# A fused state-space and expert kernel: the first block's taps move to the row queue, GpSimd takes part of the first statistics, and the first centring moves ahead of the reciprocal

## The chip, the cores and the metric

The kernel runs on one core of one Trainium2 chip. The metric is the time of one execution on the device in microseconds, as the median of several runs. The core has five instruction streams that matter here: TensorE (PE, with its weight loads as PEld), VectorE (DVE), ScalarE (ACT), GpSimd (POOL) and SyncE (SP). They wait for each other through semaphores only. DMA transfers are issued by SP, ACT and POOL, each into a queue of its own, and are carried out by 16 DMA engines.

## The reference

The input x has 8 sequences of 4096 positions with 512 channels, in float32. Two residual layers follow each other:

```
x = x + attn(layernorm(x))      # a causal convolution along the sequence, per channel, plus x * omega
x = x + ffn(layernorm(x))       # eight low-rank experts with an exact gelu, two picked for each token
```

The convolution's taps are worked out from five small parameter arrays (delta, alpha, beta, gamma, omega). A layer norm subtracts the row's mean and divides by the square root of its variance plus 1e-5. The kernel needs the first layer norm's mean and variance of all 32768 rows, while it then works through the channels 16 at a time. The stretch before that work can begin is what this document is about.

## The kernel before

The rows stand in SBUF as 128 positions within a chunk (partitions) by 256 (sequence, chunk) pairs by channels. The kernel goes through them in two halves g = 0 and 1 of 128 pairs each. A half has 32 blocks i of 16 channels, a block two units k of 8 channels; eight blocks make a tile of 128 channels. Between the halves lies the expert stage.

**The front part** ends when PE starts the first unit of g = 0. Four things happen in it side by side.

- SP loads the first 128 pairs with all 512 channels as 64 row loads of 512 KB (two pairs each, line 717, the first eight at line 700) into a ring of eight buffers. Row load n is issued once both readers have freed buffer n - 8: DVE's `bn_stats` (line 1103, two for each load, semaphore `s_free`) and POOL's copy of the first 128 channels, `keep(n)` (line 458, `s_keep`).
- ACT and PE work out 32 tables of taps and decays, which ACT stores to `taps_d` and `decay_d` in DRAM (lines 913 and 915). When the last has landed, ACT itself issues two loads for block 0: the taps (line 936, 256 KB, into `wide`) and the decays (line 937, 128 KB, into `dk`). For the later blocks `load_weights` does this on SP (lines 735 and 737).
- POOL works out the rest of the routing (`routing_rest`, three small instructions after each `keep` from n = 16 on) and issues eight of 64 tiny scatters (`send`, line 466) after the odd n from 49 to 63.
- DVE turns the 128 columns of `bn_stats` results into mean and variance: `statistics`, eight dependent instructions (lines 1144 to 1151, semaphore `s_dv`).

**What follows in order on each engine.** On ACT: `reverse(0, 0, 0)` and `reverse(0, 1, 0)`, two copies each (lines 975 and 976), which wait for block 0's taps; `lower(0, 0, 0)` (line 982); a dummy square root that loads the table (line 998); `deviations(0)`, the square root over the variances (line 941, after `s_dv` has reached 8); a dummy that loads the exponential's table (line 1000); then the first `carry` (line 952) and, once PE's first product is there, `shift_s` (line 956). ACT takes them strictly in that order:

```
            act.wait_ge(s_late, NLATE)
            for k in range(2):
                reverse(0, k, 0)
            lower(0, 0, 0)
            act.activation(spare[:, 1:2], eps[:], ACT.Sqrt)
            deviations(0)
```

On DVE: the reciprocal of the deviations (line 1226), `centre(0, 0, 0)` (line 1235, DVE's half of subtracting the mean; POOL does the other half at line 582), `stage(0, 0, 0)` (line 1246, times the reciprocal), then `centre(0, 0, 1)`, `stage(0, 0, 1)`, `centre(0, 1, 0)` and the first scan (line 1273). On PE: `chunk` (line 1458), `local` (line 1471), and from the second unit on `between` (line 1483). `stage` of unit u waits until `local` of unit u - 2 has finished with the buffer. On POOL: the first `centre`, `place_decays(0)` (line 535, waits for block 0's decays), a `send`, the second `centre`, the clearing of a buffer and another `send`, then the third `centre`, which also waits for the first scan. On SP: once the last `keep` is done, taps and decays of blocks 1 to 4, the decays of block 4 after `place_decays(0)`, and behind them the loads of the next tile (line 680).

Of the kernel before, what the change touches and what calls it, by code (L numbers as in the profile page):

```python
# [16 lines left out]
ALU = mybir.AluOpType  # L17
# [3 lines left out]
P = 128  # L21
# [27 lines left out]
def build(nc, x, delta, alpha, beta, gamma, omega, ew, ei, w1a, w1b, w2a, w2b, out, ei_experts=8):  # L49
    B, L, D = x.shape  # L50
# [10 lines left out]
    NK = D // KD  # L61
    SB = KD // 2
# [5 lines left out]
    LR = 2  # L68
    LBUF = 8
    TB = 4  # L70
    WB = 4
    NL = P // LR
# [38 lines left out]
    with ctx:  # L111
# [3 lines left out]
        def sem(name):  # L115
            return ctx.enter_context(nc.semaphore(name))
# [74 lines left out]
        w1bs = wb_row[:, KC * ER:].rearrange("p (k f) -> p k f", k=2)  # L191
        act_h = cen_row.rearrange("p (k f t) -> p k f t", k=2, t=QT)
# [72 lines left out]
        s_dv = sem("s_dv")  # L265
        s_std = sem("s_std")
# [63 lines left out]
        DV_STATS = 9  # L330
        SENT = 8
# [64 lines left out]
        def _(pool):  # L396
# [118 lines left out]

            rest = routing_rest()
            for n in range(NL):
                keep(n)
                if n == LBUF - 1:
                    pool.memset(wb[:, 0, :, :, 0:2 * ZR], 0.0).then_inc(s_late, 1)  # L520
                    pool.memset(near[:], 0.0).then_inc(s_late, 1)
                    pool.memset(shift_s[:], 0.0).then_inc(s_late, 1)
                if n >= 2 * LBUF:
                    for _ in range(3):
                        next(rest, None)
                if n >= NL - 2 * SENT and n % 2 == 1:
                    send((n - (NL - 2 * SENT)) // 2)

# [139 lines left out]
        def _(sp):  # L668
# [50 lines left out]
            sp.wait_ge(s_keep, NL)  # L719
# [80 lines left out]
            def tiles(g):  # L800
                t0 = g * DG
                if g == 0:
                    for k in range(1, WB):
                        load_weights(k, k)
                tile(g, t0, True, False)
                for t in range(t0 + 1, t0 + DG - 1):
                    tile(g, t, False, False)
                tile(g, t0 + DG - 1, False, True)
# [70 lines left out]
        def _(act):  # L879
# [49 lines left out]
            act.wait_ge(s_tab, 16)  # L929
            for k in range(TB):  # L930
                act.wait_ge(s_tapd[k], 16 * (NK // TB))
            act.wait_ge(s_dec, 16 * NK)
            for k in range(1):
                row = taps_d[k:k + 1].rearrange("k s i d -> k (s i d)")
                src = bass.AP(row.tensor, row.offset, [[2, ZR], [2 * (P + ZR), SB], [1, 2 * P]])
                act.dma_start(taps_in[k * ZR:(k + 1) * ZR], src).then_inc(s_w[k], 16)
                act.dma_start(dk[:, k, :], decay_d[k:k + 1].rearrange("k s n d -> (k s) (n d)")).then_inc(s_dk[k], 16)

            def deviations(g):
                act.wait_ge(s_dv, (g + 1) * DV_STATS - 1)  # L940
                act.activation(rstd[:, g * P:(g + 1) * P], var[:, g * P:(g + 1) * P], ACT.Sqrt,
                               bias=eps[:, 0:1]).then_inc(s_std, 1)
# [149 lines left out]
        def _(dve):  # L1092

            stats1 = wb_row[:, KC * ER:KC * ER + 6 * P].rearrange("p (r f) -> p r f", f=6)

# [36 lines left out]
            def statistics(g, st_of):  # L1132
# [9 lines left out]
                st = st_of.rearrange("p r f -> p f r")  # L1142
                m, v, r = (a[:, g * P:(g + 1) * P] for a in (mean, var, rstd))
# [79 lines left out]
            for _ in statistics(0, stats1):  # L1223
                pass
            dve.wait_ge(s_std, 1)
            dve.reciprocal(rstd[:, 0:P], rstd[:, 0:P]).then_inc(s_dv, 1)
            dve.wait_ge(s_dv, DV_STATS)

# [58 lines left out]
            dve.wait_ge(s_late, NLATE)  # L1287
            centre(0, 0, 0)
            stage(0, 0, 0)
# [354 lines left out]
```

## Time and profile before

| | us |
|---|---|
| median of 3 runs | 1125.89 |
| lowest and highest | 1124.06, 1131.58 |
| the profiled execution's own time | 1135.82 |
| its span | 1134.0 |
| first `local` product of PE begins at | 116.18 |

A time in a row is counted from the span's start. In the timeline a row gives start, duration, engine, line, operation, what is written from what, and in brackets how long the engine sat idle before and what ended that. A `q` behind an engine's name marks its sequencer, which issues DMA transfers.

### The profile page before, as it was taken

What the parts mean: (1) busy time and instruction counts of PE and PEld (TensorE: products, weight loads), DVE (VectorE), ACT (ScalarE), POOL (GpSimd) and SP (SyncE); (2) the same over time, 40 slices, a digit from 0 to 9 for tenths busy, and PEclk for the clock granted to TensorE, in tenths of its full rate; (3) what the DMA queues carried; (4) which work ended last, traced back from release to release, by engine and by line L of the source; (5) the groups of instructions that cost most, each with busy time, mean ns of one, the idle gap of its engine ahead of it and who ended that gap; (6) DMA issues with size and microseconds to landing.
All of it is one profiled execution on the core that took longest, in us unless ns stands there. A gap on an engine that the chain in (4) does not pass through costs nothing. (4 is left out here: it accounts for less than half of the span.)

```text
span 1134.0 us, 32989 instructions
## 1 busy us (share of the span) xinstructions
PE 930.9 (82%) x11452; PEld 750.8 (66%) x11452; DVE 817.4 (72%) x1360; ACT 783.8 (69%) x1151; POOL 605.4 (53%) x706
## 2 busy tenths in 40 slices
PE   3760888888688689999999999999988888886882
PEld 2540776767577567777777777777767777775771
DVE  7978998979689324576766666766757989896891
ACT  3872898979689544656565656565667989897890
POOL 5625986858483225566566656665655323332330
PEclk9995999989989898999999999999998999899896
DMA  9998999999999794999998879898839999999976
GB/s 319 394 401 298 260 248 241 274 233 295 289 295 317 217 277 110 278 258 293 264 271 221 236 207 234 228 232 218 207 80 267 231 220 273 244 308 291 307 173 150
DMA packets 392137, 288.01 MB, mean 254 GB/s; under 512 B 125928, under 2 KB 339592, under 8 KB 391554
## 3 DMA queue, kind: packets, MB, share of 16 engines
q1 hardware_dynamic: 348098, 212.21, 69.8%
q0 software_dynamic: 19520, 36.26, 14.6%
q10 hardware_dynamic: 24448, 38.61, 10.1%
q8 instruction: 43, 0.70, 0.3%
q14 instruction: 28, 0.23, 0.1%
HBM read 197.41 MB, written 100.61 MB: 263 GB/s over the span
## 5 line engine op out<-in xcount | busy, mean ns | idle before, releaser
L1471 PE MATMUL ps<-xn,wb 128*128 128x128 f32 x2048 | 275.7, 290 | 0.0
L1071 ACT ACTIVATE cen<-ps 128x1024 f32<-128x1024 f32 x156 | 155.9, 1023 | 168.8 <-PE ps L1566 161.6
L1471 PEld LDWEIGHTS ps<-xn,wb 128*128 128x128 f32 x2048 | 250.7, 200 | 17.4 <-issue 3.1
L582 POOL TENSOR_TENSOR cen<-xb,mean 128x512 f32<-128x512 f32 x128 | 142.9, 1117 | 219.4 <-DVE state L1273 166.7
L1246 DVE TENSOR_TENSOR xn<-cen,rstd 128x1024 f32<-128x1024 f32 x128 | 174.5, 1363 | 49.1 <-POOL cen L582 37.9
L1566 PE MATMUL ps<-carry,wb 64*128 64x256 f32 x1248 | 172.6, 402 | 16.0 <-DVE carry L1319 8.5
L1458 PE MATMUL ps<-xn,near 128*32 128x128 f32 x2048 | 87.9, 292 | 117.7 <-DVE xn L1246 71.9
L1581 PE MATMUL ps<-cen,xn 128*64 128x128 f32 x2496 | 160.9, 276 | 1.9 <-ACT cen L1071 1.8
L1581 PEld LDWEIGHTS ps<-cen,xn 128*64 128x64 f32 x2496 | 136.2, 137 | 39.3 <-ACT cen L1071 28.0
L1257 DVE TENSOR_TENSOR xb<-xb,ps 128x1024 f32 (+1 forms) x128 | 152.9, 1195 | 8.3 <-PE ps L1483 8.3
L975 ACT ACTIVATE wb<-wide 32x1024 f32<-32x1024 f32 x126 | 144.4, 1146 | 15.5 <-DMA wide<-taps_d 12.9
L1566 PEld LDWEIGHTS ps<-carry,wb 64*128 64x128 f32 x1248 | 116.3, 190 | 46.5 <-issue 36.0
L1458 PEld LDWEIGHTS ps<-xn,near 128*32 128x32 f32 x2048 | 52.8, 114 | 140.9 <-issue 66.7
L976 ACT ACTIVATE wb<-wide 32x768 f32<-32x768 f32 x126 | 114.8, 911 | 1.5
L614 POOL DMA_INDIRECT wide<-y_d,pick_g x78 | 86.9, 1114 | 46.6 <-POOL pick_g L611 34.6
L466 POOL DMA_INDIRECT slot_d<-rowf,posi x64 | 104.7, 1636 | 11.9 <-issue 11.9
L1303 DVE BATCH_NORM_STATS2 tstat<-wide 128x6 f32<-128x512 f32 x78 | 53.1, 690 | 76.0 <-DMA wide<-y_d,pick_g 75.4
L1235 DVE TENSOR_TENSOR cen<-xb,mean 128x512 f32<-128x512 f32 x128 | 90.2, 704 | 12.4 <-DMA xb<-L_attn_x 12.3
L1483 PE MATMUL ps<-state,carry 32*128 32x128 f32 x2048 | 94.2, 298 | 0.0
L1103 DVE BATCH_NORM_STATS2 wb<-xb 128x512 f32 (+1 forms) x128 | 80.0, 682 | 17.9 <-DMA xb<-L_attn_x 17.2
L1483 PEld LDWEIGHTS ps<-state,carry 32*128 32x128 f32 x2048 | 69.7, 188 | 25.7 <-issue 24.7
L956 ACT ACTIVATE shift_s<-ps,coef 128x124 f32<-128x124 f32 x128 | 45.4, 355 | 57.8 <-PE ps L1458 56.8
(173 smaller groups left out, 1272.6 us busy)
## 6 DMA issues: line engine op xcount, KB each, us to landing
xb<-L_attn_x SPq DMA_DIRECT2D x160, 512.0 KB, 10.1
out<-xb SPq DMA_DIRECT2D x72, 512.0 KB, 6.3
xb<-L_attn_x ACTq DMA_DIRECT2D x128, 256.0 KB
out<-xb SPq DMA_DIRECT2D x88, 256.0 KB, 4.6
wb<-L_ffn_w_B SPq DMA_DIRECT2D x78, 256.0 KB
wide<-taps_d SPq DMA_DIRECT2D x63, 256.0 KB
dk<-decay_d SPq DMA_DIRECT2D x63, 128.0 KB
out<-y_d SPq DMA_DIRECT2D x4, 1536.0 KB, 12.8
```

The lines of the kernel that those rows point to most:

```text
L466: pool.indirect_dma_start(out=slot_d, out_offset=bass.IndirectOffsetOnAxis(ap=pos_col[:, c:c + 1], axis=0), in_=row_col[:, 2 * c:2 * c + 2 ...
L582: pool.tensor_tensor(cen[:, k, 0:QB // 2].rearrange("p b r d -> p r b d"), unit_view(pool, g, i, k)[:, :, 0:UC // 2] .rearrange("p r (b d) ...
L975: act.activation(dst[0:ZR], src, ACT.Copy)
L976: act.activation(dst[ZR:2 * ZR, :, :, ZR:P], src[:, :, :, 0:P - ZR], ACT.Copy).then_inc(s_rev, 1)
L1071: act.activation(act_h[:, b % 2].rearrange("p f t -> p (f t)"), ps[:, 2 * (b % 2):2 * (b % 2) + 2, :].rearrange("p a t -> p (a t)"), ACT.G ...
L1246: dve.tensor_tensor(xn[:, k].rearrange("p (b d) r -> p b d r", d=2), cen[:, k].rearrange("p b r d -> p b d r"), rstd[:, g * P:(g + 1) * P] ...
L1257: dve.tensor_tensor(view, view, ps[:, QB * k:QB * k + QB, 0:2 * P] .rearrange("p b (d r) -> p r b d", d=2), ALU.add).then_inc(s_ev, 1)
L1458: ins = pe.matmul(ps[b * 2 * N:(b + 1) * 2 * N, QB * k, 2 * P:3 * P], near[:, h, k * QB + b, d:d + 2, :].rearrange("p z n -> p (z n)"), xn ...
L1471: ins = pe.matmul(ps[:, QB * k + b, d * P:(d + 1) * P], wb[:, h, k * QB + b, d, :], xn[:, k, 2 * b + d, :], start=(b > 0 and d == 0), stop ...
L1483: ins = pe.matmul(ps[:, QB * k + b, d * P:(d + 1) * P], carry[rows, k, d * P:(d + 1) * P], state[rows, k, :], start=False, stop=True, skip ...
L1566: ins = pe.matmul(ps[:, 2 * (b % 2) + h, f * QT:(f + 1) * QT].rearrange("p (a t) -> p a t", a=2), w1bs[half_rows, k, c * P:(c + 1) * P], r ...
L1581: ins = pe.matmul(ps[h * RANK:(h + 1) * RANK, 4, 0:P], w2as[:, (f // 2) * (FC // 2) + 2 * b + f % 2, :], act_h[:, b % 2, f, side * P:(side ...
```

## The change

It does four things. ACT no longer issues block 0's two loads; SP's `load_weights` takes block 0 too, and SP no longer waits for the last `keep` before the four pairs of loads but behind them, in front of the next tile's loads. POOL does the eight instructions of the statistics for the first 112 pairs (`first_rows`, after `keep(58)`), and DVE's `statistics(0)` covers the last 16. The eight scatters move from after the odd n of 49 to 63 to after the odd n of 41 to 55. On DVE `centre(0, 0, 0)` stands in front of the wait for the square root and the reciprocal. ACT's square root waits for `first_rows` too.

```diff
+        NHALF = 8
+        SPL = 7 * P // 8
+        SEND0 = 5 * NL // 8
...
+            def first_rows():
...
+                st = stats1[:, 0:SPL, :].rearrange("p r f -> p f r")
+                m, v, r = (a[:, 0:SPL] for a in (mean, var, rstd))
+                pool.wait_ge(s_free, SPL // LR)
+                chain(pool.tensor_tensor(m, st[:, 1, :], st[:, 4, :], ALU.add))
+                chain(pool.tensor_scalar(m, m, 0.5, None, ALU.mult))
+                chain(pool.tensor_tensor(r, st[:, 1, :], st[:, 4, :], ALU.subtract))
+                chain(pool.tensor_tensor(r, r, r, ALU.mult))
+                chain(pool.tensor_scalar(r, r, D / 4.0, None, ALU.mult))
+                chain(pool.tensor_tensor(r, r, st[:, 2, :], ALU.add))
+                chain(pool.tensor_tensor(r, r, st[:, 5, :], ALU.add))
+                chain(pool.tensor_scalar(v, r, 1.0 / D, None, ALU.mult))
...
             for n in range(NL):
                 keep(n)
+                if n == SPL // LR + 2:
+                    first_rows()
...
-                if n >= NL - 2 * SENT and n % 2 == 1:
-                    send((n - (NL - 2 * SENT)) // 2)
+                if SEND0 <= n < SEND0 + 2 * SENT and n % 2 == 1:
+                    send((n - SEND0) // 2)
...
-            sp.wait_ge(s_keep, NL)
             for k in range(TB):
                 sp.wait_ge(s_tapd[k], 16 * (NK // TB))
...
                 if g == 0:
-                    for k in range(1, WB):
+                    for k in range(WB):
                         load_weights(k, k)
+                    sp.wait_ge(s_keep, NL)
...
-            act.wait_ge(s_tab, 16)
-            for k in range(TB):
-                act.wait_ge(s_tapd[k], 16 * (NK // TB))
-            act.wait_ge(s_dec, 16 * NK)
-            for k in range(1):
-                row = taps_d[k:k + 1].rearrange("k s i d -> k (s i d)")
-                src = bass.AP(row.tensor, row.offset, [[2, ZR], [2 * (P + ZR), SB], [1, 2 * P]])
-                act.dma_start(taps_in[k * ZR:(k + 1) * ZR], src).then_inc(s_w[k], 16)
-                act.dma_start(dk[:, k, :], decay_d[k:k + 1].rearrange("k s n d -> (k s) (n d)")).then_inc(s_dk[k], 16)
...
             def deviations(g):
                 act.wait_ge(s_dv, (g + 1) * DV_STATS - 1)
+                if g == 0:
+                    act.wait_ge(s_half, NHALF)
...
-            for _ in statistics(0, stats1):
+            for _ in statistics(0, stats1, SPL):
                 pass
-            dve.wait_ge(s_std, 1)
-            dve.reciprocal(rstd[:, 0:P], rstd[:, 0:P]).then_inc(s_dv, 1)
-            dve.wait_ge(s_dv, DV_STATS)
...
+            dve.wait_ge(s_half, NHALF)
             centre(0, 0, 0)
+            dve.wait_ge(s_std, 1)
+            dve.reciprocal(rstd[:, 0:P], rstd[:, 0:P]).then_inc(s_dv, 1)
+            dve.wait_ge(s_dv, DV_STATS)
             stage(0, 0, 0)
```

## Rows read from the trace of the kernel before

**Rows 1.** The page, part 1: busy time, share of the span and instructions.

```profile
PE 930.9 (82%) x11452; PEld 750.8 (66%) x11452; DVE 817.4 (72%) x1360; ACT 783.8 (69%) x1151; POOL 605.4 (53%) x706
```

**Rows 2.** Busy time by windows, 100 to 110 us; last three columns: PEclk, DMA share, GB/s.

```profile
100.00:110.00 10.00, 0.00 (x0) 0.00 (x0) 9.50 (x19) 2.90 (x4) 6.25 (x10) 0.50 0.58 197
```

**Rows 3.** Waits: ACT from 80 to 125 us, DVE from 110 to 360 us.

```profile
ACT wb L975 <- DMA wide<-taps_d: 12.9, 1, 12.9
ACT rstd L941 <- DVE var L1151: 8.4, 1, 8.4
...
DVE cen L1235 <- DMA xb<-L_attn_x: 6.7, 1, 6.7
```

**Rows 4.** Timeline of ACT at the end of the front part.

```profile
89.73 0.33 ACTq L936 DMA_DIRECT2D wide<-taps_d  x1
...
96.69 1.13 ACT L975 ACTIVATE wb<-wide 32x1024 f32<-32x1024 f32 x1 [12.93 <-DMA wide<-taps_d]
...
102.75 0.20 ACT L998 ACTIVATE spare<-eps 128x1 f32<-128x1 f32 x1
...
111.32 0.40 ACT L941 ACTIVATE rstd<-var,eps 128x128 f32<-128x128 f32 x1 [8.37 <-DVE var L1151]
```

**Rows 5.** Timeline of DVE in the same stretch.

```profile
102.19 6.31 DVE L1103 BATCH_NORM_STATS2 wb<-xb 128x512 f32 x10 [0.25 <-DMA xb<-L_attn_x]
...
108.54 0.38 DVE L1144 TENSOR_TENSOR mean<-wb 128x128 f32<-128x128 f32 x1
...
111.06 0.23 DVE L1151 TENSOR_SCALAR var<-rstd 128x128 f32<-128x128 f32 x1
...
111.82 0.95 DVE L1226 RECIPROCAL rstd<-rstd 128x128 f32<-128x128 f32 x1 [0.54 <-ACT rstd L941]
...
113.69 1.22 DVE L1246 TENSOR_TENSOR xn<-cen,rstd 128x1024 f32<-128x1024 f32 x1
...
114.83 1.58 DVE L1235 TENSOR_TENSOR cen<-xb,mean 128x512 f32<-128x512 f32 x1
...
118.20 0.42 DVE L1273 TENSOR_TENSOR_SCAN state<-carry,shift_s 128x128 f32<-128x128 f32 x1
...
120.00 1.51 DVE L1246 TENSOR_TENSOR xn<-cen,rstd 128x1024 f32<-128x1024 f32 x1 [1.38 <-POOL cen L582]
```

**Rows 6.** Timeline of PE in its first and second unit.

```profile
115.17 1.08 PE L1458 MATMUL ps<-xn,near 128*32 128x128 f32 x16 [33.82 <-DVE xn L1246]
...
116.18 3.25 PE L1471 MATMUL ps<-xn,wb 128*128 128x128 f32 x16
...
120.59 2.05 PE L1471 MATMUL ps<-xn,wb 128*128 128x128 f32 x16
```

**Rows 7.** Timeline of POOL: a routing sum, a scatter, the last keep, two centrings.

```profile
35.53 0.46 POOL L486 TENSOR_TENSOR carry<-carry 128x128 f32<-128x128 f32 x1 [4.40 <-DVE xn L1212]
...
105.25 0.97 POOL L466 DMA_INDIRECT slot_d<-rowf,posi  x1 [0.32 <-issue]
...
107.12 0.40 POOL L458 COPY xb<-xb 128x256 f32<-128x256 f32 x1 [0.48 <-DMA xb<-L_attn_x]
...
111.46 1.10 POOL L582 TENSOR_TENSOR cen<-xb,mean 128x512 f32<-128x512 f32 x1 [2.65 <-DVE var L1151]
...
118.77 1.09 POOL L582 TENSOR_TENSOR cen<-xb,mean 128x512 f32<-128x512 f32 x1 [0.23 <-DVE state L1273]
```

**Rows 8.** DMA, 88 to 98 us: ACT's queue (packets, MB, share of 16 engines); row loads.

```profile
q10 hardware_dynamic: 508, 0.47, 15.7%
...
xb<-L_attn_x SPq DMA_DIRECT2D x6, 512.0 KB, 10.0
```

**Rows 9.** DMA, 107.5 to 113.5 us: packets, MB and rate.

```profile
DMA packets 1277, 1.19 MB, mean 198 GB/s; under 512 B 120, under 2 KB 1277, under 8 KB 1277
```

**Rows 10.** Timeline of SP: the last row loads, and the next tile's first loads.

```profile
80.94 17.09 SPq L717 DMA_DIRECT2D xb<-L_attn_x  x11
...
113.49 4.39 SPq L680 DMA_DIRECT2D xb<-L_attn_x  x4
```

More of the change, by code:

```diff
@@ L191, in build @@
         w1bs = wb_row[:, KC * ER:].rearrange("p (k f) -> p k f", k=2)
+        stats1 = wb_row[:, KC * ER:KC * ER + 6 * P].rearrange("p (r f) -> p r f", f=6)
         act_h = cen_row.rearrange("p (k f t) -> p k f t", k=2, t=QT)
@@ L265, in build @@
         s_dv = sem("s_dv")
+        s_half = sem("s_half")
         s_std = sem("s_std")
@@ L514, in routing_rest, with chain @@
                 assert n == NROUTE, n
+            def first_rows():
+                n = 0
+                def chain(ins):
+                    nonlocal n
+                    n += 1
+                    ins.then_inc(s_half, 1)
+                    pool.wait_ge(s_half, n)
+                st = stats1[:, 0:SPL, :].rearrange("p r f -> p f r")
[9 more added lines that the diff above has]
+                chain(pool.tensor_scalar(v, r, 1.0 / D, None, ALU.mult))
+                assert n == NHALF, n
             rest = routing_rest()
@@ L1092, in _ @@
         def _(dve):
-            stats1 = wb_row[:, KC * ER:KC * ER + 6 * P].rearrange("p (r f) -> p r f", f=6)
             def row_stats(q, bufs=range(LBUF)):
@@ L1130, in keep2, with statistics @@
                                 ring2[:, i:i + 2, 0:P]).then_inc(s_free2, 1)
-            def statistics(g, st_of):
+            def statistics(g, st_of, r0=0):
                 n = g * DV_STATS
@@ L1140, in chain @@
                     dve.wait_ge(s_dv, n)
-                st = st_of.rearrange("p r f -> p f r")
-                m, v, r = (a[:, g * P:(g + 1) * P] for a in (mean, var, rstd))
+                st = st_of[:, r0:, :].rearrange("p r f -> p f r")
+                m, v, r = (a[:, g * P + r0:(g + 1) * P] for a in (mean, var, rstd))
                 yield chain(dve.tensor_tensor(m, st[:, 1, :], st[:, 4, :], ALU.add))
```

## The prediction

> **What bounds the kernel now.** I began with the page. PE is busy for 82% of the span and no engine is above that [rows 1], so the long stages are loops in which engines take turns, and the change doesn't touch them. It touches the stretch before PE's first product, in which PE waits: what counts is how early that product and the loop behind it begin.
>
> The windows come next. From 100 to 110 us DVE is busy for 9.5 of 10 us, PE for none, and the DMA share has dropped to 0.58 [rows 2]: the row loads run out in this window. The waits then say who holds whom. ACT waited 12.9 us for block 0's taps and later 8.4 us for the variances [rows 3]. Both are idle time of an engine that wasn't the bound: ACT had slack of 8.4 us. The timelines give the chain that set the end. The last row load landed at 107.12, when POOL's last keep could start [rows 7]. DVE's last five loads took it from 102.19 to 108.50 without a pause, the eight statistics instructions to 111.29, ACT's square root came at 111.32, the reciprocal ended at 112.77, the first `stage` began at 113.69 [rows 4, 5], PE's `chunk` at 115.17 and its `local` at 116.18 [rows 6]. The rule of the old chain is rows, statistics, root, reciprocal, centring, stage. What the taps do is not on it: ACT got them at 96.69 and had finished everything in front of the square root at 102.95 [rows 4].
>
> **The change part by part.**
>
> *Block 0's taps behind the rows.* This is the part that decides. The last row load is issued at about 98.0 (80.94 plus 17.09) [rows 10], and in SP's queue the taps come next. Row loads land 10.0 us after their issue (median), with eight in the queue [rows 8], so what is put behind them waits for them. Two numbers are needed, when the rows end and how long the taps take after that. Taking the 384 KB of taps and decays out from between the rows gives the rows time back: ACT's queue held 15.7% of the 16 engines over 10 us, that is 1.57 us, for 0.47 MB of which this pair is 0.39 [rows 8], so 1.3 us, 1.6 at most. I take 1.4: the rows end at 105.7. The taps are two thirds of the pair, 0.9 us by the same row and 1.3 us at the 198 GB/s of the stretch that held mostly such transfers (256 KB by 198; its first microsecond was nearly empty, so this is a bound from above) [rows 9]. I take 1.0. The taps land at 106.7, with 105.9 and 107.6 as the nearer bounds.
>
> From there ACT's order counts. From the first `reverse` to the end of the dummy square root it took 102.95 minus 96.69, 6.26 us [rows 4], and the diff leaves that order alone. So the square root can't start before 106.7 + 6.3 = 113.0, against 111.32 before: 1.7 us later. ACT's 8.4 us of slack are used up and the taps are now on the chain.
>
> *Statistics.* On DVE eight instructions over 128 columns took 2.75 us (108.54 to 111.29) [rows 5]; over 16 columns they take between nothing and that. DVE's last `bn_stats` ends 1.4 us after the last row, at 107.1, so the variances stand between 107.1 and 109.9. Either is more than 3 us before 113.0: whatever is saved here, up to 2.75 us, is worth nothing, since ACT isn't there yet. If the taps were early it would be worth all of it.
>
> *POOL's eight instructions.* The trace shows none of this form. The nearest is a two-input sum of 128 elements at 0.46 us [rows 7]; with an estimated 0.08 us between dependent ones I take 0.54 each and 4.3 us in all. From above, the centring of 512 elements takes 1.10 us [rows 7], so 8.8 us. From below, 0: the work is wholly added on POOL, so a gain is excluded. `first_rows` starts after `keep(58)`, five loads before the last, at about 99.5, and ends at 103.8; queued behind it are five keeps of 0.4 us, done at 106.2 after the last row. Nobody waits for these five but the first centrings and SP's next tile. At 8.8 us the keeps end at 110.4, and POOL's centring (1.1 us) at 111.5, still ahead of the first `stage` at 114.5. The cover is ACT's chain; POOL's addition costs something from about 11 us on. The Trainium skill, GPSIMD Engine Reference, section Engine selection, puts two-input elementwise work on GpSimd at about twice VectorE's time. By that the five two-input instructions would take 0.76 us each from DVE's 0.38 [rows 5] and the eight together some 6 us, which the same cover hides. The trace has 0.46 against 0.38 for as many elements [rows 5, 7], nearer to equal, so I stay with 4.3; no sum here depends on it.
>
> *The new waits.* ACT waits for POOL's part, ready at 103.8 to 108.3; behind it stand the square root and the first `carry`, which ACT reaches at 113.0. DVE waits for it before the first centring. Neither costs anything.
>
> *The eight scatters* take 0.97 us each on POOL [rows 7]. Moved earlier by eight loads, they each delay one keep by about a microsecond; a buffer comes free only with DVE's two `bn_stats` as well, which end some 1.3 us after the landing (6.31 us for five loads [rows 5]). So the row loads are not held up. Gone from POOL's tail, they make room for `first_rows`. The last scatter also stood between the last keep and the centring, a place that waited for the variances anyway. Nothing.
>
> *First centring ahead of the reciprocal.* Before, root to stage was 111.32 to 113.69, 2.37 us. Now only the root with its hand-over (0.50), the reciprocal (0.95) and a gap of 0.04 are left, 1.49 us [rows 4, 5]: the centring, which filled nearly all of the 0.92 us between the reciprocal's end and the `stage`, is done while DVE waits for ACT. A gain of 0.9 us.
>
> *SP.* It issues its eight transfers from 96.6 on, not behind the last keep, and none of them stands in front of a row. The wait for the last keep now stands before the next tile's loads, which began at 113.49 [rows 10] behind `place_decays(0)`; that comes about 1.5 us earlier. The only long wait of DVE for such loads up to 360 us is one of 6.7 us [rows 3], two tiles later and behind a release that moves with the loop, so this is worth nothing.
>
> **The sum.** First `stage` at 113.0 + 1.5 = 114.5, that is +0.8 us. PE's first `chunk` and `local` follow by as much: `local` runs 3.25 us (this is at a granted clock of 0.50, the 1.2 GHz level, after 33.8 us of idleness; the same 16 products later take 2.05) [rows 2, 6] and ends at 120.2. But the loop didn't hang on PE there. DVE's second centring took 1.58 us beside POOL's [rows 5], where the changed POOL is done before, so it should fit into the 0.9 us that the first one had. DVE then reaches the first scan at about 118.3, near the old 118.20. POOL's third centring follows it at 118.8 and ends at 119.9, as before [rows 7]. The third `stage` stood at 120.00 [rows 5], held by that centring; it must also wait for `local`, now 120.2. So of +0.8 us at the first product +0.2 us is left in the loop, and nothing later takes or gives more. The profiled execution (1135.82, span 1134.0) would become 1136.0. It is 9.9 us above the median; nothing in the front part depends on that, so I put the same +0.2 on the median: 1126.1 us.
>
> **Rivals.**
> - *The taps come early.* If they don't wait for the rows, they land as ACT's did, 7.0 us after their issue [rows 4], at about 103.6. The root starts at 109.9, the variances' upper bound, and the third `stage` about 2.4 us earlier: 1123.5. For it speaks that a transfer of ACT's overtook row loads queued before it; against it, that this was another queue. The Trainium skill, DMA: Bandwidth & Descriptors, section Queues, rings and completion order, has each engine switch between queues, but take one queue's descriptors in ring order. That speaks for the forecast; this trace shows the overtaking between queues only.
> - *The rows gain nothing, the slower side.* If rows end at 107.1 as before, because the last engines to finish had other small work, the taps land at 108.1, the root starts at 114.4, PE's first `local` ends at 121.6 and the third `stage` slips by 1.6 us: 1127.5. It decides from a landing past 106.7 on, each microsecond costing one. For it speaks that the DMA share is only 0.58 in the last window [rows 2], so some engines lag, whatever lies between.
> - *The loop settles otherwise.* A shifted start meets the tile loads at another phase; the one 6.7 us wait [rows 3] could grow or shrink by some 4 us: 1122 or 1130.
> - *Over 1%.* None of the mechanisms reaches 11 us. All of the front part's waits at stake add up to less than 9.
>
> **How the numbers follow.** Forecast (landing 105.9 to 107.6, from -0.6 to +1.1 us) 55%, taps early 14%, rows gain nothing 17%, loop otherwise 11% (half each way), over 1% 3%. About 1% is what a measurement of this kernel can tell from no change. The range takes in the first three cases with the spread of the runs shown (1.8 below the median and 5.7 above) and part of the fourth: 1122.5 to 1130.0. Faster by over 1%: 0.01; within 1%: 0.97; slower: 0.02.
>
> **What would show it.** In the profile after: ACT's first line 975 waits for the taps until 106 to 107.6 and the square root starts 6.3 us behind; DVE's last statistics end before 110 and DVE then sits idle for 3 us or more until the reciprocal; POOL's eight instructions take 4 to 9 us and nobody waits; root to `stage` 1.5 us; PE's first `chunk` between 115.2 and 117. I am wrong if line 975 starts before 105, if POOL's centring is what the first `stage` waits for, or if the loop's start and the total move by different amounts.

## The result

The changed kernel is slower by half a per cent: 1131.91 us against 1126.95 us (medians of 20 runs each), ratio 1.0051 with a 95% interval from 1.0037 to 1.0064. In microseconds the ratio is +5.7, from 4.2 to 7.2; the two medians are 5.0 apart. I had forecast +0.2 us and a range whose upper end, 1130.0, the median has left.

The profiled execution of the changed kernel has a span of 1129.4 us, less than the 1134.0 of before. Single executions differ by more than the effect: the stretch of the experts between the halves alone is some 12 us shorter in this execution than in that of before (432 against 444 us, by the first and last of their products). So the two spans can't be compared, but the front parts can, step by step. The timeline of ACT in the changed kernel, in the form of [rows 4]:

```profile
110.73 1.13 ACT L997 ACTIVATE wb<-wide 32x1024 f32<-32x1024 f32 x1 [28.24 <-DMA wide<-taps_d]
...
116.80 0.20 ACT L1020 ACTIVATE spare<-eps 128x1 f32<-128x1 f32 x1
116.91 0.39 ACT L963 ACTIVATE rstd<-var,eps 128x128 f32<-128x128 f32 x1
```

Block 0's taps let ACT begin at 110.73, where I had 106.7 and where 96.69 stood before [rows 4]. From there to the end of the dummy square root it is 6.27 us, as forecast, and the root starts at 116.91, 5.6 us later than before. DVE in the same stretch, in the form of [rows 5]:

```profile
110.10 1.29 DVE L1123 BATCH_NORM_STATS2 wb<-xb 128x512 f32 x2 [0.89 <-DMA xb<-L_attn_x]
...
112.93 0.17 DVE L1171 TENSOR_SCALAR var<-rstd 128x16 f32<-128x16 f32 x1
113.14 0.69 DVE L1252 TENSOR_TENSOR cen<-xb,mean 128x512 f32<-128x512 f32 x1
...
117.33 0.95 DVE L1308 RECIPROCAL rstd<-rstd 128x128 f32<-128x128 f32 x1 [3.50 <-ACT rstd L963]
...
118.32 1.22 DVE L1263 TENSOR_TENSOR xn<-cen,rstd 128x1024 f32<-128x1024 f32 x1
...
124.52 1.23 DVE L1263 TENSOR_TENSOR xn<-cen,rstd 128x1024 f32<-128x1024 f32 x1 [2.18 <-PE ps L1492]
```

The statistics are done at 113.10 and DVE then waits 3.5 us for ACT's root. The first `stage` is 4.63 us late and the third, from which the loop runs, 4.52 us. But the last `bn_stats` pair also starts only at 110.10: the rows themselves are late. POOL shows that best, since its keep of a row load starts as the load lands:

```profile
85.39 0.40 POOL L463 COPY xb<-xb 128x256 f32<-128x256 f32 x1
...
105.58 0.40 POOL L463 COPY xb<-xb 128x256 f32<-128x256 f32 x1 [0.38 <-DMA xb<-L_attn_x]
...
107.83 0.40 POOL L463 COPY xb<-xb 128x256 f32<-128x256 f32 x1 [1.85 <-DMA xb<-L_attn_x]
...
110.00 0.40 POOL L463 COPY xb<-xb 128x256 f32<-128x256 f32 x1 [1.77 <-DMA xb<-L_attn_x]
```

The first of these is keep 48, the last keep 63. Before, the last one started at 107.12 [rows 7]; I had put it at 105.7. The last three are 2.2 us apart, where DVE's five loads of [rows 5] had come every 1.26 us. So two things went wrong at once: the rows end 4.3 us later than forecast, and the taps behind them with them.

### The profile page after: what moved, and what is told of

Read it like the earlier page. It is cut to its first block and busy times, and to the rows that moved or that the text cites. A ratio compares the mean times of both kernels' runs of the same rounds, so it can differ in the third digit from the quotient of the medians.

```text
span 1129.4 us, 32996 instructions
## 1 busy us (share of the span) xinstructions
PE 925.3 (82%) x11452; PEld 748.0 (66%) x11452; DVE 814.9 (72%) x1360; ACT 786.2 (70%) x1151; POOL 605.5 (54%) x714
## 5 line engine op out<-in xcount | busy, mean ns | idle before, releaser
L1587 PE MATMUL ps<-carry,wb 64*128 64x256 f32 x1248 | 170.0, 402 | 12.8 <-DVE carry L1340 12.2
L1587 PEld LDWEIGHTS ps<-carry,wb 64*128 64x128 f32 x1248 | 113.3, 190 | 42.7 <-issue 23.6
L471 POOL DMA_INDIRECT slot_d<-rowf,posi x64 | 96.9, 1514 | 11.9 <-issue 11.9
```

What stands on the lines that cost most here:

```text
L471: pool.indirect_dma_start(out=slot_d, out_offset=bass.IndirectOffsetOnAxis(ap=pos_col[:, c:c + 1], axis=0), in_=row_col[:, 2 * c:2 * c + 2 ...
L1587: ins = pe.matmul(ps[:, 2 * (b % 2) + h, f * QT:(f + 1) * QT].rearrange("p (a t) -> p a t", a=2), w1bs[half_rows, k, c * P:(c + 1) * P], r ...
```

## The experiments

Theory 1, crowding: not all DMA engines finish the rows at the same time. Those that are done go on to the four pairs of taps and decays in the same queue, and in doing so slow down the row packets of those that lag. Theory 2: the rows are late because of another part of the change, the earlier scatters or POOL's eight instructions. Behind both stands what I had forecast, the place of the taps in the queue and ACT's order.

What makes theory 1 possible is seen in the kernel before. Its DMA from 102 to 109 us, in 40 slices of 0.175 us (busy tenths, then rate):

```profile
DMA  9999997644433343222222112101000000000663
GB/s 410 410 374 352 375 340 293 247 165 176 164 141 118 120 142 129 94 94 94 105 82 82 70 70 82 59 0 5 2 0 0 0 0 0 0 0 0 105 47 111
DMA packets 583, 0.89 MB, mean 126 GB/s; under 512 B 130, under 2 KB 175, under 8 KB 583
## 3 DMA queue, kind: packets, MB, share of 16 engines
q1 hardware_dynamic: 487, 0.88, 35.9%
q0 software_dynamic: 96, 0.00, 1.1%
```

From 103.2 on, the share falls step by step. It is down to 0.4 at 103.4, while the last packet of a row starts at 106.5 and the last row load lands just before 107.12. So most engines are done some three microseconds before the last one. In the changed kernel the same stretch reads:

```profile
DMA  9999998999999999999999999999999999999986
GB/s 187 164 164 164 123 158 146 222 310 269 193 158 181 158 158 135 181 199 205 193 240 275 240 240 205 217 199 240 222 263 252 217 228 228 211 211 211 170 164 146
DMA packets 1302, 1.41 MB, mean 201 GB/s; under 512 B 101, under 2 KB 1128, under 8 KB 1302
## 3 DMA queue, kind: packets, MB, share of 16 engines
q1 hardware_dynamic: 1302, 1.41, 109.0%
```

All engines are busy, at half the rate that they had a moment before (381 GB/s from 98 to 100 us). A packet took 1.09 x 16 x 7.0 us / 1302 = 94 ns in the mean for 1.08 KB; before, the same sum (with both queues' 37.0%) gives 71 ns for 1.53 KB. Packets that carry less take longer: the engines are held up within them. The trace also keeps each packet with its size: a row goes in packets of 2 KB, taps and decays in packets of 1 KB. In the changed kernel the first packet of 1 KB behind the rows starts at 100.9 us and the last one of a row at 108.8, so the two do run side by side. And a row packet between 102 and 109 us took 162 ns in the mean, against 86 ns before.

**The front part's own spread.** Single profiles are compared below, so the kernel before was profiled once more.

> The kernel before, profiled once more, to learn how far the front part itself differs between two executions. If the rows' supply is steady, keep 48 starts at 84.4 and the last keep at 107.1 as in the first profile, within 0.3 us; if it is not, every comparison of single front parts carries that spread (the four kernels above had keep 48 at 84.8 to 85.5), and the distance from keep 48 to the last keep, 22.8 us before, is the better measure of crowding.

Its keep 48 started at 85.54 and its last keep at 108.16, both one microsecond later than in the first profile, and its third `stage` at 121.04. The distance between the two keeps was 22.62 us against 22.76. So times of single front parts carry about 1 us, and the distance from keep 48 to the last keep is what crowding is read from.

**Block 0 back on ACT.** The changed kernel with:

```diff
+            sp.wait_ge(s_keep, NL)               # ahead of SP's pairs, as before
...
-                    for k in range(WB):
+                    for k in range(1, WB):
                         load_weights(k, k)
-                    sp.wait_ge(s_keep, NL)
...
+                act.dma_start(taps_in[k * ZR:(k + 1) * ZR], src).then_inc(s_w[k], 16)
+                act.dma_start(dk[:, k, :], ...).then_inc(s_dk[k], 16)
```

> The changed kernel with one part undone: ACT issues block 0's taps and decays again as soon as the tables have landed, and SP waits for the last keep before the pairs of blocks 1 to 3. POOL's 112 columns, the earlier scatters and the first centring ahead of the reciprocal stay. Theory 1 (crowding: the four pairs queued behind the rows run on the DMA engines that have finished their rows and slow down the engines that lag): the last keep starts at 106.5 to 107.3 as before, ACT's first line 975 at 96 to 98, the variances stand at 110.3, the square root follows at once, the first stage at 111.8 (1.9 us earlier than before), and the total is 1.5 to 2.5 us below before (ratio 0.998). Theory 2 (the rows end late because of the earlier scatters or POOL's statistics): the last keep stays at 109 to 110, the first stage comes at 114 or later, total 0 to 1 us above before.

The distance was 22.48 us, so theory 2 falls: the earlier scatters and POOL's instructions are all in this kernel and the rows come as before. The variances decided again and the root followed them at once:

```profile
111.15 0.40 ACT L973 ACTIVATE rstd<-var,eps 128x128 f32<-128x128 f32 x1 [8.75 <-DVE var L1181]
```

The first `stage` was 0.76 us earlier than before in a front part whose rows came 1.2 us later. Against keep 48 that is a gain of 1.9 us, but at the third `stage` only 1.0 us of it is left, because the second `stage` had to wait for POOL's second centring. In the total nothing shows: ratio 1.0011, from 0.9988 to 1.0034. I had expected 1.5 to 2.5 us below before, and the interval holds 1.4 us at most: that forecast failed.

**One pair behind the rows.** The changed kernel with:

```diff
-                    for k in range(WB):
+                    load_weights(0, 0)
+                    sp.wait_ge(s_keep, NL)
+                    for k in range(1, WB):
                         load_weights(k, k)
-                    sp.wait_ge(s_keep, NL)
```

> The changed kernel with only block 0's pair queued directly behind the rows; SP waits for the last keep before the pairs of blocks 1 to 3. Theory 1, with the crowding done by the three pairs that nobody needs yet: the last keep at 106 to 107, the taps at 107 to 108, the square root 6.3 us later at 113.3 to 114.3, the third stage 0 to 1 us later than before, total 0 to 1.5 us above before. If block 0's pair alone does the crowding, or theory 2 holds: the last keep at 109 or later, taps at 110 or later, the third stage 3 us or more later, total 3 to 5 us above before.

The last keep came at 107.36, the distance was 22.52 us, ACT began at 108.25 and the root at 114.42. The third `stage` was 1.4 us later than in the first profile of before and 0.4 us later than in the second; the ratio was 1.0027, from 1.0002 to 1.0052. I had expected the last keep by 107, the third `stage` at most 1 us later and the total at most 1.5 above before (measured +3.0, from 0.2 to 5.9), so all came out on the far side. The three pairs that nobody needs yet account for 2.1 us of the changed kernel's distance. But block 0's pair alone already used up what taking it from between the rows gives back: the distance is that of before, not 1.4 us less. This is, nearly to the number, the rival that the rows gain nothing.

**This part alone.** The kernel before with ACT's two loads removed, all four pairs on SP and the wait for the last keep behind them:

```diff
-            sp.wait_ge(s_keep, NL)
...
-                    for k in range(1, WB):
+                    for k in range(WB):
                         load_weights(k, k)
+                    sp.wait_ge(s_keep, NL)
```

> The kernel before with only this part of the change: all four pairs on SP directly behind the rows, the wait for the last keep behind them. DVE does all 128 columns, the scatters stay at n = 49 to 63, the centring stays behind the reciprocal. Theory 1: the last keep at 109.5 to 110.5, taps at 110.5 to 111.5, the square root at 117 to 118, the first stage at 119.3 to 120.3 (0.9 later than in the changed kernel), the total 5 to 7 us above before (ratio 1.005 to 1.006). Theory 2: the last keep at about 105.7, the taps at 107, the total 1 to 2 us above before.

Last keep 110.42, distance 24.99 us, ACT from 111.66, root at 117.84, first `stage` at 120.04, ratio 1.0060 (1.0037 to 1.0083). That is within or next to every bound that I had set. The taps' place by itself gives the whole loss. At the third `stage`, 126.36 against 124.52 in the changed kernel, the other parts of the change give 1.8 us back by single profiles; in the total the two intervals overlap, and no gain of theirs is shown.

**Three pairs behind the rows, block 0 on ACT.** This has the crowding without the late taps:

```diff
+                act.dma_start(...)               # block 0's two loads, on ACT as before
...
-                    for k in range(WB):
+                    for k in range(1, WB):
                         load_weights(k, k)
                     sp.wait_ge(s_keep, NL)
```

> The changed kernel with block 0's pair on ACT again, but the pairs of blocks 1 to 3 still queued directly behind the rows. It separates crowding from the lateness of the taps. Theory 1: the last keep at 108.5 to 110 although the taps come at 97; ACT is ready at 103, so the variances decide: the square root at 111.7 to 113, the first stage at 113.2 to 114.5, total -0.5 to +1 us against before. Without crowding it is the same as the kernel with all of SP's pairs behind the keep: last keep at 107, first stage at 111.8, 2 us below before.

```profile
96.04 1.13 ACT L1007 ACTIVATE wb<-wide 32x1024 f32<-32x1024 f32 x1 [13.01 <-DMA wide<-taps_d]
...
114.13 0.40 ACT L973 ACTIVATE rstd<-var,eps 128x128 f32<-128x128 f32 x1 [11.82 <-DVE var L1181]
```

ACT had its taps at 96.04 and waited 11.8 us for the variances: the last keep started at 110.98, 25.68 us after keep 48. Both were later than my bounds. The distance is 3.2 us more than in the first experiment, from which this kernel differs only in SP's wait. The ratio was 1.0041, from 1.0021 to 1.0061. I had expected the total between 0.5 below and 1 us above before; it was +4.6, from 2.4 to 6.9. Crowding alone, without late taps, costs nearly as much as the whole change.

**What crowds.** The taps differ from the rows in three ways: all engines read the same 10 KB of DRAM over and over, a piece is 1 KB, and a transfer is written into 32 partitions only. Four kernels take these apart. The first reads other data:

```diff
-                    for k in range(WB):
-                        load_weights(k, k)
+                    for k in range(WB):          # 256 KB each out of x, every KB once
+                        far_src = bass.AP(x.tensor, 7 * L * D + k * ZR * SB * 2 * P, ...)
+                        sp.dma_start(taps_in[k * ZR:(k + 1) * ZR], far_src).then_inc(s_w[k], 16)
+                        sp.dma_start(dk[:, k, :], dec).then_inc(s_dk[k], 16)
```

> The changed kernel, but the four taps transfers behind the rows read 256 KB each from a far part of x, every KB once, instead of the overlapping windows over 10 KB that make up a block's taps. Sizes, destinations and order stay. Block 0 to 3 of the first half then get wrong taps: that part of the computation is left out. Theory 1a (what crowds the lagging rows is that all engines read the same few KB of DRAM at once): from keep 48 to the last keep 20.5 to 22.5 us (after: 24.6), the stretch from 101 to 109 moves 300 GB/s or more at a DMA share of 1.0 until the fast engines are done, the taps land at 107 to 108 and the square root comes 2 to 3 us earlier than in the changed kernel. Theory 1b (it is the size of 1 KB or the 32 partitions written): nothing changes, 24 to 25 us and about 220 GB/s.

It got worse, not better: distance 25.59 us, last keep 111.71, ACT from 112.40. It also changed more than I had meant. The windows lie side by side in x and went as packets of 8 KB, as this line from 102 to 109 us shows (663 packets, 578 of them under 8 KB):

```profile
DMA packets 663, 1.41 MB, mean 201 GB/s; under 512 B 91, under 2 KB 368, under 8 KB 578
```

So neither the shared source nor the small piece is needed for crowding. The second loads the decays behind the rows and the taps after the last keep:

```diff
                     for k in range(WB):
-                        load_weights(k, k)
+                        sp.dma_start(dk[:, k, :], dec).then_inc(s_dk[k], 16)
                     sp.wait_ge(s_keep, NL)
+                    for k in range(WB):
+                        sp.dma_start(taps_in[k * ZR:(k + 1) * ZR], src).then_inc(s_w[k], 16)
```

> The changed kernel with only the four decay transfers (128 KB each, every KB read once, all 128 partitions written, also in pieces of 1 KB) directly behind the rows, and the four taps transfers after the last keep. Theory 1a: decays don't crowd; from keep 48 to the last keep 20.5 to 22 us, the last keep at 105.5 to 106.5; the taps of block 0 are issued after it and land some 2.7 us later at 108.5 to 109.5, the square root 6.3 us behind, the third stage 1.5 to 2.5 us later than before. If the piece size of 1 KB does the crowding, the distance is 23 us or more.

The distance was 20.80 us, 1.9 us less than before: with no taps anywhere near the rows, they end that much sooner. The last keep itself started at 107.30 and not at 105.5 to 106.5, as keep 48 was late too (86.50). The taps, now issued after it, let ACT start 3.8 us behind it and not 2.7, so the third `stage` came 4.3 us later than in the first profile of before, where I had 1.5 to 2.5. The mean packet from 102 to 109 us, from these two lines, took 0.483 x 16 x 7.0 / 915 = 59 ns for 1.26 KB:

```profile
DMA packets 915, 1.15 MB, mean 164 GB/s; under 512 B 93, under 2 KB 617, under 8 KB 915
## 3 DMA queue, kind: packets, MB, share of 16 engines
q1 hardware_dynamic: 913, 1.15, 48.3%
```

A row packet took 86 ns in the mean, as in the kernel before. So pieces of 1 KB don't crowd either. The third is this kernel with the decays' transfers reading the taps' overlapping windows:

```diff
-                sp.dma_start(dk[:, k, :], dec).then_inc(s_dk[k], 16)
+                hot_src = bass.AP(row.tensor, row.offset, [[2, P], [1, 2 * P]])
+                sp.dma_start(dk[:, k, :], hot_src).then_inc(s_dk[k], 16)
```

> The kernel of the decays-early experiment with one thing changed: the four transfers behind the rows (128 KB each, 128 partitions written) now read overlapping windows of 1 KB out of a block's 10 KB of taps, as the taps transfers do. The decays of blocks 0 to 3 of the first half are wrong with it: that part is left out. Reading the same few KB against reading apart, with the partitions written held at 128. If only the 32 partitions of the destination crowd (theory 1c): as with the decays, 20.8 us from keep 48 to the last keep and row packets as before. If the shared source has a part of its own: 22 us or more.

20.93 us: reading the same few KB costs the rows nothing. (These 128 windows, 8 bytes apart, lie within 2 KB of a block's taps, closer together than those of the taps transfers, which cover 10 KB.) The fourth is the kernel with another source, its megabyte sent as one transfer over 128 partitions instead of four over 32:

```diff
-                        sp.dma_start(taps_in[k * ZR:(k + 1) * ZR], far_src).then_inc(s_w[k], 16)
+                    sp.dma_start(taps_in, all_src).then_inc(s_w[0], 16)
```

Three transfers of 0.2 KB after the last keep take over the semaphores of blocks 1 to 3.

> The experiment with another source (four transfers of 256 KB out of x into 32 partitions each) with one thing changed: the same megabyte into the same places as one transfer over all 128 partitions, ahead of the decays. The taps of blocks 0 to 3 of the first half stay wrong: that part is left out. Theory 1c (a transfer into 32 partitions can only use part of the way into SBUF, all engines press on it, and the lagging row packets that need the same part wait): from keep 48 to the last keep 20.5 to 22 us instead of 25.6, and the window 102 to 109 moves 260 GB/s or more instead of 201. If the amount of data behind the rows does the crowding, whatever its shape: 25 us again.

The distance fell from 25.59 to 21.05 us. From 102 to 109 us, the windows of the two (last three columns: clock, DMA share, GB/s), four transfers first:

```profile
102.00:109.00 7.00, 0.00 (x0) 0.00 (x0) 3.70 (x6) 0.00 (x0) 3.98 (x9) 0.50 1.06 201
```

```profile
102.00:109.00 7.00, 0.00 (x0) 0.00 (x0) 6.51 (x16) 0.34 (x1) 3.76 (x9) 0.50 0.70 267
```

Its packets in the same window, 119 of them of 8 KB:

```profile
DMA packets 894, 1.87 MB, mean 267 GB/s; under 512 B 92, under 2 KB 588, under 8 KB 775
```

The same bytes from the same place to the same place: with one transfer the DMA engines moved a third more in two thirds of the busy time, and DVE was busy for 6.51 of 7 us instead of 3.70. The packets themselves say it most directly. In this window a row packet took 175 ns in the mean beside the four transfers and 88 ns beside the one, which is what it takes undisturbed; a packet of 8 KB took 643 ns and 316 ns. Besides the width, two things differ: the four transfers became one, and it stands ahead of all decays. The decays of the second kernel are four transfers in a row over 128 partitions and slowed no row packet, so their number isn't it. What crowds is that a transfer writes into 32 partitions. The Trainium skill, SBUF — State Buffer, section Door 1: the DMA port swizzle, states that partitions 0 to 31, and 0 to 63 as well, are reached through 8 of 16 ports only, about 218 GB/s at best. The 201 GB/s here agree with it. Its rule is what I had not weighed: blocks 0 and 1 lie in partitions 0 to 63, and by it the lagging rows' packets into those have to pass the same ports. That this is what slows the rows is not shown. A packet's record doesn't name its partitions, and in the kernel with one pair all 78 row packets that start between 102.0 and 103.5 us took 122 ns or more, though only block 0's 32 partitions were being written narrowly there.

**A version that keeps what is good.** In the first experiment POOL's second centring held the second `stage`. Two more scatters ahead should clear it:

```diff
-        SENT = 8
-        SEND0 = 5 * NL // 8
+        SENT = 10
+        SEND0 = 9 * NL // 16
```

> The changed kernel with block 0's taps on ACT and SP's wait as before (as the first experiment here), and two more scatters moved ahead: ten after the odd n of 37 to 55, so that POOL has none between its first two centrings. In the first experiment POOL's second centring was what the second stage waited for (1.6 us) and it gave back the 0.8 us won at the first stage. Expected: POOL's second centring ends 1.2 us or more before the second stage needs it, the third stage 0.8 to 1.5 us earlier than in the first experiment, total 0.5 to 1.5 us below it and 0 to 1.5 us below before (ratio 0.999 to 1.000). If the third stage hangs on local's end (PE at half clock), the gain is 0.5 us at most.

```profile
113.33 1.85 POOL L471 DMA_INDIRECT slot_d<-rowf,posi  x1 [0.16 <-issue]
...
115.21 1.11 POOL L612 TENSOR_TENSOR cen<-xb,mean 128x512 f32<-128x512 f32 x1
...
116.42 1.23 DVE L1273 TENSOR_TENSOR xn<-cen,rstd 128x1024 f32<-128x1024 f32 x1 [1.57 <-POOL cen L612]
```

It didn't: the loop of POOL's first centrings issues a scatter of its own between them, whichever number it bears, and the second `stage` waited 1.57 us for POOL as in the first experiment. Moving the start of the list only changes which scatter that is. I had read the code wrongly. The third `stage`, at 119.97, came 0.2 us earlier than in the first experiment and not 0.8 to 1.5. Ratio 1.0001, from 0.9981 to 1.0021.

The last version adds what the decays showed, all four decay transfers behind the rows:

```diff
-            sp.wait_ge(s_keep, NL)
...
-                act.dma_start(dk[:, k, :], ...)      # block 0's decays leave ACT
...
-                    for k in range(1, WB):
-                        load_weights(k, k)
+                    for k in range(WB):
+                        sp.dma_start(dk[:, k, :], dec).then_inc(s_dk[k], 16)
+                    sp.wait_ge(s_keep, NL)
+                    for k in range(1, WB):
+                        sp.dma_start(taps_in[k * ZR:(k + 1) * ZR], src).then_inc(s_w[k], 16)
```

> A version that keeps what the runs speak for: block 0's taps on ACT between the rows, all four decay transfers on SP directly behind the rows (they did not crowd), the taps of blocks 1 to 3 after the last keep, ten scatters ahead, POOL's 112 columns and the first centring ahead of the reciprocal. Expected: from keep 48 to the last keep 22.0 us instead of 22.4 (128 KB less between the rows), everything up to the third stage 0.3 to 0.6 us earlier than with ten scatters alone, the total 0 to 1.5 us below before (ratio 0.9985 to 1.000). If the decays of block 0 land too late for POOL's second centring, the third stage comes no earlier and the ratio is 1.000.

The distance was 22.28 us (22.40 with ten scatters alone), the root started at 110.62 and the third `stage` at 119.60, 0.4 us earlier than in the first profile of before. The ratio was 1.0001, from 0.9967 to 1.0035. Its interval ends just below the one of the changed kernel, which begins at 1.0037. So it is better than the changed kernel and not told apart from the kernel before; nothing tried here is shown to beat that one.

All front parts together (us from the span's start; "ACT's first 975" is the first `reverse`, line 975 of the kernel before; the distance is from keep 48 to the last keep; ratios where several rounds were run):

| kernel | keep 48 | last keep | distance | ACT's first 975 | root | third stage | ratio |
|---|---|---|---|---|---|---|---|
| before | 84.36 | 107.12 | 22.76 | 96.69 | 111.32 | 120.00 | |
| before, again | 85.54 | 108.16 | 22.62 | 96.29 | 112.36 | 121.04 | |
| changed | 85.39 | 110.00 | 24.61 | 110.73 | 116.91 | 124.52 | 1.0051 |
| block 0 on ACT | 85.53 | 108.01 | 22.48 | 96.14 | 111.15 | 120.14 | 1.0011 |
| one pair behind | 84.84 | 107.36 | 22.52 | 108.25 | 114.42 | 121.43 | 1.0027 |
| this part alone | 85.43 | 110.42 | 24.99 | 111.66 | 117.84 | 126.36 | 1.0060 |
| three pairs behind | 85.30 | 110.98 | 25.68 | 96.04 | 114.13 | 123.12 | 1.0041 |
| other source | 86.12 | 111.71 | 25.59 | 112.40 | 118.58 | 125.64 | |
| decays behind | 86.50 | 107.30 | 20.80 | 111.11 | 117.28 | 124.28 | |
| shared source, 128 partitions | 85.26 | 106.19 | 20.93 | 109.84 | 116.02 | 122.98 | |
| one transfer, 128 partitions | 85.11 | 106.16 | 21.05 | 108.66 | 114.83 | 122.54 | |
| ten scatters | 85.44 | 107.84 | 22.40 | 95.93 | 110.98 | 119.97 | 1.0001 |
| decays behind, ten scatters | 85.19 | 107.47 | 22.28 | 94.82 | 110.62 | 119.60 | 1.0001 |

## Why the prediction was wrong

**The step that failed** is the one on SP: that its eight transfers begin early and "none of them stands in front of a row". In the order of the queue that is so. But a queue is served by 16 engines that aren't at the same place in it, and a transfer behind the rows runs beside the lagging rows as soon as the first engine is through. I had the sign of this in hand, the DMA share of 0.58 in [rows 2], and used it only to say that some engines lag, not to ask what they would then have beside them. The price: the distance from keep 48 to the last keep became 24.61 us. I had forecast 21.4 (22.76 less 1.4), so 3.2 us were missing.

**The gain from taking the pair out of the rows** was right and even undersized: 1.4 us forecast, 1.9 shown with the decays alone behind the rows. With one pair behind the rows the crowding spent it again and left 22.52 us.

**The time of the taps behind the rows** I took as 1.0 us. ACT started 0.7 us after the last keep's start (110.00 to 110.73) and 0.9 us after it with one pair. The number came out, but not for the reason given. I had the taps' whole transfer begin when the rows end. Its first packets ran at 100.9 us, eight microseconds before the last one of a row, and what came after the last row was only the rest. That it comes to about 1 us is luck.

**ACT's order** held: 6.27 us against 6.26. The new chain, rows, taps, ACT's copies, root, was the one named; only its first link was misplaced, by 4.0 us.

**The statistics** gained 1.1 of the 2.75 us that were the upper bound, and it was worth nothing, as argued: 1.7 us for DVE's 16 columns (111.42 to 113.10), with ACT not there until 116.91. POOL's eight instructions took 4.5 us in the changed kernel (99.94 to 104.40) against 4.3 forecast, and nobody waited. But the term came out by luck in part. I had taken POOL for nearly as fast as DVE. Like for like, the five instructions with two inputs took 2.37 us for 112 columns, against 1.81 us for 128 on DVE before, which is 1.5 times as long per element. That lies between my near equality and the twice of the prediction's other estimate, whose 6 us were too long. The three with one input took 1.49 against 0.69 us, 2.5 times as long. What hid this is that only 112 columns were worked on.

```profile
99.94 0.53 POOL L534 TENSOR_TENSOR mean<-wb 128x112 f32<-128x112 f32 x1
...
103.91 0.49 POOL L541 TENSOR_SCALAR var<-rstd 128x112 f32<-128x112 f32 x1
```

**The centring ahead of the reciprocal** held: root to `stage` 1.41 us against 1.49 forecast and 2.37 before.

**The loop's start** held in form. The third `stage` waited for PE's `local` (2.18 us, in the row above), which came later and, with 3.68 us, ran longer than the 3.25 of [rows 6]:

```profile
120.80 3.68 PE L1492 MATMUL ps<-xn,wb 128*128 128x128 f32 x16
```

**SP** issued its eight transfers from 97.84 on, where I had 96.6. The next tile's first load came at 115.78 and not some 1.5 us before 113.49. Ahead of it stands block 4's pair, whose taps can be loaded only once ACT has read block 0's out of the same buffer: SP waited 8.7 us for ACT there and issued that pair from 114.92 on. I had put the lateness of the taps on ACT's chain, but not on this one.

**From the front part to the total.** The third `stage` was later by 4.5 us against the first profile of before and by 3.5 against the second, the total by 5.7, from 4.2 to 7.2. The other kernels that lost time show the same small surplus: one pair 1.4 or 0.4 against +3.0, three pairs 3.1 or 2.1 against +4.6. It lies within the intervals and the spread of single profiles. From the third `stage` to the experts' first product it was 279.0 and 279.5 us in the two profiles of before, 282.2 in the changed kernel, but 277.3 with this part alone. So single profiles can't say whether the later stages, the later loads of the next tile among them, add about a microsecond of their own. It is left open.

**The rivals.** That the rows gain nothing was the one nearest to what happened, and its price of 1.6 us is what the experiment with one pair shows at the third `stage` (1.4). In the changed kernel the rows didn't merely gain nothing, they lost 1.9 us. That the taps come early fell: they came last. That the loop settles otherwise was priced at some 4 us either way; beyond the surplus just told, nothing here speaks for it or against it. Why my chances left out what happened: the lateness of the rows had a floor at before's 107.1 in my mind, because nothing was in front of them.

**The signs that I had named.** Of those, ACT's wait until 106 to 107.6, the end of DVE's statistics before 110 and the first `chunk` before 117 failed (110.73, 113.10 and 119.79), all for the late rows. The square root 6.3 us behind ACT's first line, DVE's idle time of 3 us or more, POOL's 4 to 9 us and the 1.5 us from root to `stage` came as said.

## What to carry to other kernels

A transfer queued behind others isn't out of their way: look at where the DMA share begins to fall before the last landing, since that is where the next transfer will already run. Ask which partitions it writes; here four into 32 partitions each pressed the rows' packets and their own to half the rate (175 against 88 ns, 643 against 316), while the same megabyte over 128 did them no harm. And before a transfer is moved from idle time of an engine to the end of a chain, look up what that engine does in order behind it; here 6.3 us of copies and table loads stood between the taps and the root that everybody waited for.

## What the runs showed of the hardware that was not expected

- Four transfers of 256 KB into 32 partitions each, behind the rows, held 16 busy engines to 201 GB/s, where the same stretch moved 267 GB/s at a share of 0.70 once the megabyte went over 128 partitions. The kernel before probably has the effect too, within the rows: taking block 0's pair out of them gave 1.9 us for 384 KB, which at the 386 GB/s that the rows reach from 98 to 102 us would be 1.0 us, and from 94 to 98 us a row packet took 100 ns in the mean there, against 88 in the changed kernel. No run tries the pair within the rows at full width.
- All engines reading overlapping windows of the same 2 KB of DRAM, for each of four transfers, did no harm: 20.93 us against 20.80 with data read once (one profile each).
- The DMA engines end one stream of equal row loads three to four microseconds apart (the share falls from 103.2 us on, and the last row packet starts at 106.5 in the kernel before and at 107.4 with block 0 back on ACT). Which engines lag, and whether the small stores of the tables make them lag, was not tried.
- The same front part differed by 1 us between two executions of one kernel: keep 48 came at 84.36 and 85.54 us.
